# P turned in 32x32 blocks on VectorE and placed by DMAs, in a convolution with 3x3 local attention

## Chip, cores and metric

The kernel runs on one core of a Trainium2 chip. The metric is the device time of one execution in microseconds. A profiled execution gives the span (first to last instruction of the core) and, beside it, its own device time.

## What is computed

The input is a batch of 16 images of 32x32 pixels with 128 channels, float32. Cut to what matters:

```python
perceived = depthwise_conv3x3(x, w_perc) + b_perc        # 3 outputs per channel
hid = gelu(w_up1 @ perceived + b_up1)                    # 256 channels
h = x + w_up2 @ hid + b_up2                              # 128 channels
q, k, v = split(h @ w_qkv.T + b_qkv)
scores[pos] = (q * shifted(k, pos)).sum(-1) * scale      # 9 neighbours, zero padded
w = softmax(scores)
out = h + sum over pos of w[pos] * shifted(v, pos)
```

## The kernel before

**Layout.** An image has 1024 pixels, 8 tiles of 128 pixels (4 rows of 32). The attention of a tile is a dense block: 128 queries on the partitions against a window of 192 keys (the tile's 4 rows and one row above and below), masked. `p_sb` holds exp(scores) for the 8 tiles, [128 queries, 8, 192 keys and a few more], and GpSimd's `normalise` (L918) multiplies half an image (4 tiles, 768 elements a partition) by the reciprocal sums. To multiply by the values, P must have its keys on the partitions: that is `pt`, [128 keys, 8 key tiles, 192 queries that see them].

**P turned.** `transpose_p(n, g)` (L406 to L418) has TensorE transpose the four middle 128x128 blocks of half g into the PSUM bank `work[:, 1 + g]`, and ScalarE's `take_pt` (L579) copies them into `pt`. VectorE's `edges(n, g)` (L781 to L793) turns the 32x32 blocks of the rows above and below, with two STREAM_TRANSPOSE instructions a half. `values(n, g)` (L420) then does 10 matmuls of `v_sb` with `pt` for half an output image, `add_h` (L795) adds h into `o_sb`, and SP stores it.

**Stages.** Each engine runs its own instruction stream, written out by hand, and semaphores order them. `steady` (L224) calls each engine's `body(n, ...)` for n = 0 to 16; five pairs of bodies are a hardware loop. In body n the convolution of image n runs (12 units on TensorE, `unit`, L339, each 9 matmuls of 256 columns), together with the up projection and the attention scores of image n-1, and the values of image n-2. In the code's counting of attention, body n calls `transpose_p(n, 0)` at its end, and body n+1 calls `transpose_p(n, 1)`, `values(n+1, 0)` after unit 0 and `values(n+1, 1)` after unit 1 (L466 to L472). Then come units 2 and 3, the up projection `up` (L365), units 4 and 5, the projections q and v, and units 6 to 11 with the scores between them. Body 16 has no convolution.

**VectorE's order** at the end of a body (L868 to L877): the reciprocal sums of half 1, `edges(n, 0)`, `combine`, `combine_y` and `finish_y` of the second conv half (L718 to L751), `edges(n, 1)`. The gelu on ScalarE waits for `finish_y`. At the start of the next body come `transform_ab`, `add_h` for half 0, `transform`, `add_h` for half 1.

**SP's order** in a body (L301): load the planes of image n+2 when the present ones are used up, load the pixel rows of image n+1 when h of this body is done, and store the two output halves. All its DMAs go through one queue in program order; a wait holds up what stands behind it.

Of the kernel before, what the change touches and what calls it, by code (L numbers as in the profile page):

```python
# [14 lines left out]
P = 128  # L15
# [65 lines left out]

def build(nc, x_planes, x_rows, w_perc, b_perc, w1_c, b_up1, w2_c, b_up2, wqk_c, wv_c, b_qkv, ident_c, ident_bf_c,
          mask_c, zero_c, out):
    with ExitStack() as ctx:
# [13 lines left out]

        ident = sb("ident", [P, P])
        ident_bf = sb("ident_bf", [P, P], BF16)  # L100
# [50 lines left out]


        pt = sb("pt", [P, T, WINDOW])
        o_sb = sb("o_sb", [P, PIX])
# [35 lines left out]
        s_ready = sem("s_ready")  # L190
        pt_ready = sem("pt_ready")
        o_ready = sem("o_ready")
# [5 lines left out]
        p_done = sem("p_done")  # L198
        pt_done = sem("pt_done")

# [10 lines left out]
        rsum_done = sem("rsum_done")  # L211
        edges_done = sem("edges_done")
        pn_last_done = sem("pn_last_done")
# [7 lines left out]
        V_PARTS = (range(0, 2), range(2, 4), range(4, 6), range(6, 8))  # L221
        N_W = 8

        def steady(eng, body, last=None):  # L224
# [42 lines left out]
        @block.sync  # L267
        def _(sp):
            def load(dst, src, **kw):
                sp.dma_start(dst, src, **kw).then_inc(weights_in, 16)  # L270

            def load_planes(n, par):
                sp.dma_start(xp[:, par, :, :, :].rearrange("p k r w -> p (k r w)"), x_planes[n]).then_inc(
                    x_loaded[par], 16)

            def load_rows(n, par):
                sp.dma_start(xr[:, par, :], x_rows[n]).then_inc(xr_loaded[par], 16)

            sp.dma_start(w1T[:, :, :].rearrange("p m d -> p (m d)"), w1_c).then_inc(first_in, 16)
            load_planes(0, 0)  # L280
            sp.dma_start(ident[:, :], ident_c).then_inc(first_in, 16)
            load(w2T[:, :], w2_c)
            load(wqk_in[:, :, :].rearrange("p j c -> p (j c)"), wqk_c)
            load(wv_in[:, :], wv_c)
            load(bqk[:, :], b_qkv[0:2 * C].rearrange("(j p) -> p j", p=P), allow_slow_non_contiguous=True)
            load(bv[:, :], b_qkv[2 * C:3 * C].partition_broadcast(P))
            load(mask_bf[:, :, :], mask_c)
            load(ident_bf[:, :], ident_bf_c)
            load(zeros[:, :, :], zero_c)
            load_planes(1, 1)  # L290
            load_rows(0, 0)
            load_rows(1, 1)

            def store_out(n):
                for g in range(2):

                    sp.wait_ge(o_done, n * 2 - 3 + g)
                    sp.dma_start(out[n - 2][:, g * CH:(g + 1) * CH],
                                 o_sb[:, g * CH:(g + 1) * CH]).then_inc(stored[g], 16)

            def body(n, par, conv, attn, store, more):  # L301
                if conv and (not isinstance(n, int) or n + 2 < B):

                    sp.wait_ge(ab_done, n * 2 + 2)
                    sp.wait_ge(fcge_done, n * 3 + 3)
                    load_planes(n + 2, par)
                if attn and (not isinstance(n, int) or n + 1 < B):

                    sp.wait_ge(h_done, n * 2)
                    load_rows(n + 1, 1 - par)  # L310
                if store:
                    store_out(n)

            steady(sp, body, last=store_out)
            for g in range(2):
                sp.wait_ge(stored[g], 16 * B)

        @block.tensor
        def _(pe):

            def small_weights():
# [9 lines left out]
                pe.wait_ge(biases_in, 48)  # L331
                pe.wait_ge(first_in, 32)
                for g in range(2):
# [71 lines left out]

            def transpose_p(n, g):  # L406
                if is_last(n) and g == 1:
                    pe.wait_ge(pn_last_done, 1)
                else:
                    pe.wait_ge(pn_done, n * 2 + (g - 1))  # L410

                if is_last(n):
                    pe.wait_ge(z_done, n * 4 - 3 if g == 0 else n * 4)
                else:
                    pe.wait_ge(z_done, n * 4 + (0 if g == 0 else -2))
                for u in range(4):
                    last = pe.transpose(work[:, 1 + g, u * P:(u + 1) * P], p_sb[:, 4 * g + u, W:W + P], ident[:, :])
                last.then_inc(pt_ready, 1)  # L418

            def values(n, g):  # L420


                pe.wait_ge(v_done, n * 4 - 4)
                pe.wait_ge(pt_done, n * 2 + (g - 3))
                pe.wait_ge(edges_done, n * 4 + (2 * g - 6))
                half = T // 2 * TR
                blocks = [(i, max(i * TR - 1, g * half), min((i + 1) * TR + 1, (g + 1) * half)) for i in range(T)]
                blocks = [(i, first, end) for i, first, end in blocks if first < end]
                for i, first, end in blocks:
                    above = i * TR - 1  # L430
                    last = pe.matmul(work[:, g, (first - g * half) * W:(end - g * half) * W], v_sb[:, i, :],  # L431
                                     pt[:, i, (first - above) * W:(end - above) * W], start=(i == blocks[0][0]),
                                     stop=(i == blocks[-1][0]), skip_group_check=True)
                last.then_inc(o_ready, 1)

            def last_attention(n):
# [14 lines left out]
                scores(n, 3)  # L451

                transpose_p(n, 0)
                values(n + 1, 0)
                transpose_p(n, 1)
                values(n + 1, 1)

            def body(n, par, conv, attn, store, more):
# [7 lines left out]
                units(0)  # L466
                if store:
                    transpose_p(n - 1, 1)
                    values(n, 0)
                units(1)  # L470
                if store:
                    values(n, 1)  # L472
                units(2)
                units(3)
# [35 lines left out]
                units(9, 10, 11)  # L510
                if attn:
                    transpose_p(n, 0)

# [3 lines left out]
        def _(act):  # L517
# [36 lines left out]
            def prime_gelu():  # L554

                nc.scalar.activation(primer[:, :], ident[:, 0:1], ACT.Gelu).then_inc(primed, 1)

            act.wait_ge(first_in, 32)
            prime_gelu()
# [18 lines left out]

            def take_pt(n, g):  # L579
                act.wait_ge(pt_ready, n * 2 + (g - 1))  # L580
                nc.scalar.copy(pt[:, 4 * g:4 * g + 4, W:W + P],
                               work[:, 1 + g, :].rearrange("p (t q) -> p t q", t=4)).then_inc(pt_done, 1)

            def body(n, par, conv, attn, store, more):
                def exp(i):
                    if i % 2 == 0:
                        act.wait_ge(rmax_done, n * 4 + (i // 2 - 3))
                    u = i % 2 * STEP
                    nc.scalar.activation(p_sb[:, i, 0:KEYS], s_bank(n, i // 2)[:, u:u + KEYS], ACT.Exp,  # L589
                                         bias=negmax[:, i:i + 1], accum_out=p_sum[:, i:i + 1]).then_inc(p_done, 1)  # L590

                if store:
                    take_pt(n - 1, 1)
                if attn:
# [25 lines left out]
                if conv:  # L620
                    prime_gelu()
                if attn:
                    take_pt(n, 0)
                if is_last(n):
                    take_pt(n, 1)

# [3 lines left out]
        def _(dve):  # L630
# [23 lines left out]
            dve.wait_ge(filters_done, 11)  # L654
            dve.wait_ge(first_in, 32)

# [123 lines left out]

            def edges(n, g):  # L781

                if is_last(n) and g == 1:
                    dve.wait_ge(pn_last_done, 1)
                else:
                    dve.wait_ge(pn_done, n * 2 + (g - 1))
                first, end = 4 * g, 4 * g + 4
                a = max(first, 1)
                nc.vector.transpose(pt[P - W:P, a - 1:end - 1, P + W:WINDOW],
                                    p_sb[0:W, a:end, 0:W]).then_inc(edges_done, 1)  # L790
                e = min(end, T - 1)
                nc.vector.transpose(pt[0:W, first + 1:e + 1, 0:W],  # L792
                                    p_sb[P - W:P, first:e, P + W:WINDOW]).then_inc(edges_done, 1)  # L793

# [30 lines left out]
            def body(n, par, conv, attn, store, more):  # L825
# [34 lines left out]
                if is_last(n):  # L860
                    edges(n, 0)
                    sums(n, 1)
                    normalise_last(n)
                    edges(n, 1)
                    add_h(n + 1, 0)
                    add_h(n + 1, 1)
                    return
                if attn:  # L868
                    sums(n, 1)
                    edges(n, 0)  # L870
                if conv:
                    combine(n, 1)
                    combine_y(n, 1)
                if conv:
                    finish_y(n, 1)
                if attn:
                    edges(n, 1)  # L877

# [105 lines left out]
```

## Time and profile before

| what | value |
|---|---|
| median of 3 runs | 500.1 us (498.7 to 500.71) |
| the profiled execution's own time | 498.68 us |
| its span | 496.9 us |
| TensorE matmul busy | 445.7 us, 90% |
| VectorE busy | 356.3 us, 72% |
| ScalarE busy | 230.5 us, 46% |
| GpSimd busy | 194.6 us, 39% |
| DMA queue of SP | 10784 packets, 29.03 MB, 17.4% of 16 engines |

Busy times are sums over the span; matmuls are pipelined, so the rate at which they start says more than how long one lasts. Rows below are read with these names: PE is TensorE's matmul, PEld its weight load, DVE VectorE, ACT ScalarE, POOL GpSimd, SPq the issuing of DMAs by SP. L431 is line 431 of the kernel before.

### The profile page before, as it was taken

The page shows a single profiled execution, that of the slowest core. Times are in us where ns is not written, and L with a number is a line of the kernel's source. Part 1 is how long each engine was busy: PE and PEld are TensorE (multiplying, and loading weights), DVE is VectorE, ACT ScalarE, POOL GpSimd, SP SyncE. Part 2 cuts the span into 40 slices and gives each one's busy share as a digit, 9 for nine tenths or more (in the row PEclk, how much of TensorE's full clock was granted, in tenths as well). Part 3 has the DMA queues.
Part 4 walks back from the last instruction along what each step waited for, and adds up shares of the span by engine and source line. Part 5 has one row for each costly group of instructions (what it writes and reads, how often), then busy time and mean ns, then how long its engine had stood idle before and what let it go on. Part 6 is the DMA issues. An engine that isn't in the chain of part 4 may idle for free.

```text
span 496.9 us, 8443 instructions
## 1 busy us (share of the span) xinstructions
PE 445.7 (90%) x2964; PEld 390.7 (79%) x2964; DVE 356.3 (72%) x728; ACT 230.5 (46%) x491; POOL 194.6 (39%) x154
## 2 busy tenths in 40 slices
PE   1558899999999999999999999999999999999984
PEld 1547588787979788787979788797979888797953
DVE  5997669677685958677685958677685958664644
ACT  2443164453627354453626444453736444461633
POOL 3565435344441525344451526344351526320201
PEclk9999899999999999999999999999999999999999
DMA  8101020303103040402104040402204020201011
GB/s 278 65 0 58 0 100 1 140 2 97 46 13 130 2 142 0 140 0 79 62 3 138 0 140 0 140 0 61 79 0 140 0 84 0 86 2 42 1 44 43
DMA packets 11509, 29.31 MB, mean 59 GB/s; under 512 B 2400, under 2 KB 3168, under 8 KB 11488
## 3 DMA queue, kind: packets, MB, share of 16 engines
q1 hardware_dynamic: 10784, 29.03, 17.4%
q8 instruction: 12, 0.20, 0.2%
q10 hardware_dynamic: 704, 0.02, 0.1%
q14 instruction: 9, 0.07, 0.1%
HBM read 20.65 MB, written 8.39 MB: 58 GB/s over the span
## 4 chain that ended last, share of the span: by engine, by line
PE 61%; DVE 21%; issue 10%; ACT 4%; DMA 1%; DVEq 1%; POOLq 0%; POOL 0%; SPq 0%; ACTq 0%
PE m_ps L359 24%; PE work L372 11%; PE s_ps L401 8%; PE work L431 6%; PE work L378 5%; PE work L383 5%; ACT p_sb L589 3%; DVE y L737 3%; DVE y L740 3%; PE s_ps L397 2%; DVE ps_sb L726 2%; DVE negmax L772 2%; DVE pt L792 2%; DVE o_sb L699 1%; DVE y L736 1%
## 5 line engine op out<-in xcount | busy, mean ns | idle before, releaser
L359 PE MATMUL m_ps<-thi,whi 128*128 128x256 f32 x576 | 187.6, 326 | 14.0 <-POOL wlo L927 6.1
L359 PE MATMUL m_ps<-tlo,whi 128*128 128x256 f32 x576 | 164.2, 285 | 0.0
L359 PE MATMUL m_ps<-thi,wlo 128*128 128x256 f32 x576 | 164.1, 285 | 0.0
L359 PEld LDWEIGHTS m_ps<-thi,whi 128*128 128x128 f32 x576 | 111.3, 193 | 22.5 <-issue 15.1
L918 POOL TENSOR_TENSOR p_sb<-p_sb,rsum 128x768 f32<-128x768 f32 x31 | 45.5, 1468 | 192.7 <-DVE rsum L779 192.7
L359 PEld LDWEIGHTS m_ps<-tlo,whi 128*128 128x128 f32 x576 | 111.6, 194 | 7.2 <-issue 7.2
L359 PEld LDWEIGHTS m_ps<-thi,wlo 128*128 128x128 f32 x576 | 111.4, 193 | 0.0
L911 POOL TENSOR_TENSOR tlo<-t,thi 128x1088 fp32r<-128x1088 f32 (+1 forms) x32 | 61.7, 1948 | 46.1 <-ACT thi L528 46.1
L589 ACT ACTIVATE p_sb<-s_ps,negmax 128x197 f32<-128x197 f32 x124 | 51.4, 423 | 37.6 <-DVE negmax L772 37.6
L606 ACT ACTIVATE q_sb<-work,bq_s 128x512 f32<-128x512 f32 x32 | 22.0, 688 | 100.2 <-PE work L378 100.1
L431 PE MATMUL work<-pt,v_sb 128*128 128x160 f32 (+2 forms) x320 | 50.5, 305 | 17.3 <-DVE pt L792 15.8
L431 PEld LDWEIGHTS work<-pt,v_sb 128*128 128x128 f32 x320 | 47.0, 190 | 20.3 <-issue 20.3
L758 DVE TENSOR_TENSOR v_sb<-work,bv 128x256 f32<-128x256 f32 x62 | 26.1, 421 | 45.2 <-PE work L383 44.9
L372 PE MATMUL work<-hid,w2T 128*128 128x512 f32 x120 | 55.7, 608 | 2.0 <-ACT hid L544 2.0
L544 ACT ACTIVATE hid<-y,b1eff 128x1024 f32<-128x1024 f32 x32 | 36.6, 1144 | 36.9 <-DVE y L750 30.9
L401 PE MATMUL s_ps<-h_around,q_sb 128*128 128x192 f32 x248 | 50.4, 326 | 0.0
L528 ACT CAST thi<-t 128x1088 fp32r<-128x1088 f32 (+1 forms) x32 | 26.3, 870 | 43.6 <-DVE t L677 43.6
L401 PEld LDWEIGHTS s_ps<-h_around,q_sb 128*128 128x128 f32 x248 | 42.2, 191 | 1.4
L372 PEld LDWEIGHTS work<-hid,w2T 128*128 128x128 f32 x120 | 22.2, 194 | 24.7 <-issue 24.7
L821 DVE SCALAR_TENSOR_TENSOR h_around<-work,b,xr 128x512 f32<-128x512 f32 x30 | 22.5, 751 | 20.7 <-PE work L372 20.7
L772 DVE TENSOR_REDUCE negmax<-s_ps 128x2 f32<-128x394 f32 x62 | 35.2, 568 | 2.1
L383 PE MATMUL work<-wvT,h_around 128*128 128x129 f32 x248 | 35.3, 275 | 0.9 <-DVE h_around L821 0.9
(110 smaller groups left out, 665.6 us busy)
## 6 DMA issues: line engine op xcount, KB each, us to landing
xp<-x_planes SPq DMA_DIRECT2D x16, 680.0 KB, 5.6
xr<-x_rows SPq DMA_DIRECT2D x16, 512.0 KB, 4.0
out<-o_sb SPq DMA_DIRECT2D x32, 256.0 KB, 4.1
w1T<-w SPq DMA_DIRECT2D x1, 384.0 KB, 3.2
mask_bf<-masks SPq DMA_DIRECT2D x1, 192.0 KB, 4.0
w2T<-w SPq DMA_DIRECT2D x1, 128.0 KB, 4.9
wqk_in<-w_qk SPq DMA_DIRECT2D x1, 128.0 KB, 4.8
ident<-identity SPq DMA_DIRECT2D x1, 64.0 KB, 4.8
```

Source lines behind the costliest of these rows:

```text
L359: last = pe.matmul(m_ps[:, b, col:col + S], a[:, j, dy, half * P:(half + 1) * P], c[:, par, T_PLACE[j], dy * WIN:dy * WIN + S], start=(s = ...
L372: last = pe.matmul(up_bank(n, c), w2T[:, half * C:(half + 1) * C], hid[:, half, c * CH:(c + 1) * CH], start=(half == 0), stop=(half == 1))
L383: last = pe.matmul(v_bank(n, part)[:, u * VT:(u + 1) * VT], h[:, i * P:(i + 1) * P], wvT[:, :], start=True, stop=True)
L401: last = pe.matmul(s[:, u, 0:WINDOW], q_sb[:, i * P:(i + 1) * P], h_around[:, i * P:i * P + WINDOW], start=False, stop=(u == 1), skip_grou ...
L431: last = pe.matmul(work[:, g, (first - g * half) * W:(end - g * half) * W], v_sb[:, i, :], pt[:, i, (first - above) * W:(end - above) * W] ...
L528: nc.scalar.copy(thi[:, par, part, :], t[:, part, :]).then_inc(thi_done, 1)
L544: nc.scalar.activation(hid[:, half, :].rearrange("p (r k s) -> p k r s", k=K4, s=WIN), y[:, half, :, :].rearrange("p k (r s) -> p k r s", ...
L589: nc.scalar.activation(p_sb[:, i, 0:KEYS], s_bank(n, i // 2)[:, u:u + KEYS], ACT.Exp, bias=negmax[:, i:i + 1], accum_out=p_sum[:, i:i + 1] ...
L758: nc.vector.tensor_tensor(v_sb[:, first:end, :], sums[:, :, 0:C], bv[:, :].unsqueeze(1).to_broadcast([P, len(tiles), C]), ALU.add).then_in ...
L772: nc.vector.tensor_reduce(negmax[:, pair], s[:, :, 0:KEYS], AX.X, ALU.max, negate=True).then_inc(rmax_done, 1)
L911: nc.gpsimd.tensor_tensor(tlo[:, par, part, :], t[:, part, :], thi[:, par, part, :].bitcast(F32), ALU.subtract).then_inc(tlo_done, 1)
L918: nc.gpsimd.tensor_tensor(p_sb[:, tiles, 0:WINDOW], p_sb[:, tiles, 0:WINDOW], rsum[:, tiles].unsqueeze(2).to_broadcast([P, 4, WINDOW]), AL ...
```

## The change

TensorE's transposes, ScalarE's copies and the identity matrix that they needed go. VectorE turns a whole half image (4 tiles, all 192 columns) in one STREAM_TRANSPOSE into a new buffer `turned`. That turns each 32x32 block in place, so the blocks stand on the partitions of their query row and not of their key row. SP then moves them with 12 DMAs a half image, each from 32 partitions of `turned` to 32 partitions of `pt`, in pieces of 32 float32. The turn of half 1 stands between `combine_y` and `finish_y`, and the edges' instructions go. The values stand one conv unit later. In SP's body the moves stand last.

```diff
-        pt_ready = sem("pt_ready")
-        pt_done = sem("pt_done")
-        edges_done = sem("edges_done")
+        turned_done = sem("turned_done")
+        pt_moved = [sem(f"pt_moved{i}") for i in range(2)]
+        MOVED = TR * 3 * 16
...
-            sp.dma_start(ident[:, :], ident_c).then_inc(first_in, 16)
...
+            def move_p(n, g):
+                sp.wait_ge(turned_done, n * 2 + (g - 1))
+                if from_image(n, 2):
+                    sp.wait_ge(o_ready, n * 2 + (g - 3))
+                for row in range(TR):
+                    for dk in range(3):
+                        shift, near = divmod(row + dk - 1, TR)
+                        first, end = max(4 * g, -shift), min(4 * g + 4, T - shift)
+                        col = (near + 2 - dk) * W
+                        sp.dma_start(pt[near * W:(near + 1) * W, first + shift:end + shift, col:col + W],
+                                     turned[row * W:(row + 1) * W, first:end, (row + dk) * W:(row + dk + 1) * W]
+                                     ).then_inc(pt_moved[g], 16)
...
                 if store:
                     store_out(n)
+                if attn:
+                    move_p(n, 0)
+                    move_p(n, 1)
...
             def values(n, g):
                 pe.wait_ge(v_done, n * 4 - 4)
-                pe.wait_ge(pt_done, n * 2 + (g - 3))
-                pe.wait_ge(edges_done, n * 4 + (2 * g - 6))
+                pe.wait_ge(z_done, n * 4 - 4)
+                pe.wait_ge(pt_moved[g], n * MOVED - MOVED)
...
                 units(0)
-                if store:
-                    transpose_p(n - 1, 1)
-                    values(n, 0)
                 units(1)
                 if store:
+                    values(n, 0)
+                units(2)
+                if store:
                     values(n, 1)
-                units(2)
                 units(3)
...
-            def edges(n, g):
+            def turn_p(n, g):
                 (waits for normalise)
+                if from_image(n, 2):
+                    dve.wait_ge(pt_moved[g], n * MOVED - MOVED)
+                tiles = slice(4 * g, 4 * g + 4)
+                nc.vector.transpose(turned[:, tiles, :], p_sb[:, tiles, 0:WINDOW]).then_inc(turned_done, 1)
...
                 if attn:
                     sums(n, 1)
-                    edges(n, 0)
+                    turn_p(n, 0)
                 if conv:
                     combine(n, 1)
                     combine_y(n, 1)
+                if attn:
+                    turn_p(n, 1)
                 if conv:
                     finish_y(n, 1)
-                if attn:
-                    edges(n, 1)
```

ScalarE's exp of the next image waits for `turned_done` where it had TensorE's order before. Three waits for `first_in` go from 32 to 16, because ident isn't loaded.

## Rows read from the trace of the kernel before

**Rows 1.** The page: span, and busy us (share) of each engine.

```profile
span 496.9 us, 8443 instructions
PE 445.7 (90%) x2964; PEld 390.7 (79%) x2964; DVE 356.3 (72%) x728; ACT 230.5 (46%) x491; POOL 194.6 (39%) x154
```

**Rows 2.** Waits: us in total, times, longest us.

```profile
PE work L431 <- DVE pt L792: 15.8, 14, 1.2
```

**Rows 3.** Order of time, TensorE around the values: start, us, what; last row merged.

```profile
302.03 0.60 PE L417 MATMUL work<-ident,p_sb 128*128 128x128 f32 x4
...
303.52 0.60 PE L417 MATMUL work<-ident,p_sb 128*128 128x128 f32 x4
...
303.96 1.50 PE L431 MATMUL work<-pt,v_sb 128*128 128x160 f32 x10
...
305.30 0.36 PE L359 MATMUL m_ps<-thi,whi 128*128 128x256 f32 x1
...
307.74 1.66 PE L431 MATMUL work<-pt,v_sb 128*128 128x32 f32 x10 [1.14 <-DVE pt L792]
...
309.39 2.13 PE m_ps L359 x18
```

**Rows 4.** Order of time, VectorE in the same stretch.

```profile
301.06 0.27 DVE L789 STREAM_TRANSPOSE pt<-p_sb 32x96 f32<-32x96 f32 x1
...
305.94 0.41 DVE L742 SCALAR_TENSOR_TENSOR y<-ru_sb 128x256 f32<-128x256 f32 x1
...
307.32 0.27 DVE L792 STREAM_TRANSPOSE pt<-p_sb 32x96 f32<-32x96 f32 x1
```

**Rows 5.** Groups by line and form: busy us, mean ns, idle before.

```profile
L789 DVE STREAM_TRANSPOSE pt<-p_sb 32x128 f32<-32x128 f32 x16 | 4.9, 304 | 0.5
...
L789 DVE STREAM_TRANSPOSE pt<-p_sb 32x96 f32<-32x96 f32 x16 | 4.3, 272 | 1.4 <-POOL p_sb L918 0.9
```

**Rows 6.** Order of time, SP's issues: start, us in issuing, what.

```profile
5.50 0.43 SPq L270 DMA_DIRECT2D zeros<-zero_keys  x1
5.97 0.43 SPq L273 DMA_DIRECT2D xp<-x_planes  x1
...
315.93 0.35 SPq L277 DMA_DIRECT2D xr<-x_rows  x1
...
344.00 0.35 SPq L277 DMA_DIRECT2D xr<-x_rows  x1
```

**Rows 7.** Issue to landing of the stores (first) and of the row loads.

```profile
DMA to landing us min/median/max: 2.0/4.1/4.7
...
DMA to landing us min/median/max: 3.5/4.0/6.7
```

**Rows 8.** Queues in 0 to 12 us: packets, MB, share of 16 engines.

```profile
q1 hardware_dynamic: 2060, 3.27, 80.8%
q10 hardware_dynamic: 704, 0.02, 3.5%
```

**Rows 9.** Granted clock in 40 slices, then order of time, TensorE in the ramp.

```profile
PEclk9999899999999999999999999999999999999999
...
21.75 0.42 PE L359 MATMUL m_ps<-tlo,whi 128*128 128x256 f32 x1
21.97 0.41 PE L359 MATMUL m_ps<-thi,wlo 128*128 128x256 f32 x1
...
43.65 0.33 PE L359 MATMUL m_ps<-tlo,whi 128*128 128x256 f32 x1
```

**Rows 10.** Order of time, TensorE in the last stages.

```profile
469.11 1.25 PE L417 MATMUL work<-ident,p_sb 128*128 128x128 f32 x8
...
472.78 1.66 PE L431 MATMUL work<-pt,v_sb 128*128 128x32 f32 x10 [0.77 <-DVE pt L792]
...
487.82 0.66 PE L417 MATMUL work<-ident,p_sb 128*128 128x128 f32 x4 [2.03 <-POOL p_sb L918]
...
491.97 1.66 PE L431 MATMUL work<-pt,v_sb 128*128 128x32 f32 x10 [0.72 <-issue]
```

**Rows 11.** Waits in the first 10 us.

```profile
DVE p_sb L690 <- DMA ident<-identity: 1.4, 1, 1.4
```

More of the change, by code:

```diff
@@ L79, in zero_keys, with build @@
     return z
-def build(nc, x_planes, x_rows, w_perc, b_perc, w1_c, b_up1, w2_c, b_up2, wqk_c, wv_c, b_qkv, ident_c, ident_bf_c,
+def build(nc, x_planes, x_rows, w_perc, b_perc, w1_c, b_up1, w2_c, b_up2, wqk_c, wv_c, b_qkv, ident_bf_c,
           mask_c, zero_c, out):
@@ L96, in build @@
         work = psum("work", 3)
-        ident = sb("ident", [P, P])
         ident_bf = sb("ident_bf", [P, P], BF16)
@@ L150, in build @@
         p_sb = sb("p_sb", [P, T, KEYS + 3])
+        turned = sb("turned", [P, T, WINDOW])
         pt = sb("pt", [P, T, WINDOW])
@@ L299, in store_out @@
                                  o_sb[:, g * CH:(g + 1) * CH]).then_inc(stored[g], 16)
+            def move_p(n, g):
[10 more added lines that the diff above has]
+                                     ).then_inc(pt_moved[g], 16)
             def body(n, par, conv, attn, store, more):
+                if isinstance(n, int) and n == 1:
+                    sp.wait_ge(zeroed, 3)
                 if conv and (not isinstance(n, int) or n + 2 < B):
@@ L331, in small_weights @@
                 pe.wait_ge(biases_in, 48)
-                pe.wait_ge(first_in, 32)
+                pe.wait_ge(first_in, 16)
                 for g in range(2):
@@ L404, in scores @@
                 last.then_inc(s_ready, 1)
[L406 to L418, printed above, removed]
             def values(n, g):
                 pe.wait_ge(v_done, n * 4 - 4)
-                pe.wait_ge(pt_done, n * 2 + (g - 3))
-                pe.wait_ge(edges_done, n * 4 + (2 * g - 6))
+                pe.wait_ge(z_done, n * 4 - 4)
+                pe.wait_ge(pt_moved[g], n * MOVED - MOVED)
                 half = T // 2 * TR
@@ L451, in last_attention @@
                 scores(n, 3)
-                transpose_p(n, 0)
                 values(n + 1, 0)
-                transpose_p(n, 1)
                 values(n + 1, 1)
@@ L510, in body @@
                 units(9, 10, 11)
-                if attn:
-                    transpose_p(n, 0)
             steady(pe, body)
@@ L554, in prime_gelu @@
             def prime_gelu():
-                nc.scalar.activation(primer[:, :], ident[:, 0:1], ACT.Gelu).then_inc(primed, 1)
-            act.wait_ge(first_in, 32)
+                nc.scalar.activation(primer[:, :], w1T[:, 0, 0:1], ACT.Gelu).then_inc(primed, 1)
+            act.wait_ge(first_in, 16)
             prime_gelu()
@@ L577, in _ @@
                     nc.scalar.mul(bqk_s[:, :], wa[:, 2 * C + 2:2 * C + 3], -SCALE).then_inc(consts_done, 1)
[L579 to L582, printed above, removed]
             def body(n, par, conv, attn, store, more):
@@ L587, in exp @@
                         act.wait_ge(rmax_done, n * 4 + (i // 2 - 3))
+                        if from_image(n, 2):
+                            act.wait_ge(turned_done, n * 2 + (i // 4 - 3))
                     u = i % 2 * STEP
@@ L590, in exp @@
                                          bias=negmax[:, i:i + 1], accum_out=p_sum[:, i:i + 1]).then_inc(p_done, 1)
-                if store:
-                    take_pt(n - 1, 1)
                 if attn:
@@ L621, in body @@
                     prime_gelu()
[L622 to L625, printed above, removed]
             steady(act, body)
@@ L654, in _ @@
             dve.wait_ge(filters_done, 11)
-            dve.wait_ge(first_in, 32)
+            dve.wait_ge(first_in, 16)
             def rows(a):
@@ L786, in edges @@
                     dve.wait_ge(pn_done, n * 2 + (g - 1))
[L787 to L793, printed above, removed]
+                if from_image(n, 2):
+                    dve.wait_ge(pt_moved[g], n * MOVED - MOVED)
+                tiles = slice(4 * g, 4 * g + 4)
+                nc.vector.transpose(turned[:, tiles, :], p_sb[:, tiles, 0:WINDOW]).then_inc(turned_done, 1)
             def add_h(n, g):
@@ L869, in body @@
                     sums(n, 1)
-                    edges(n, 0)
+                    turn_p(n, 0)
                 if conv:
@@ L873, in body @@
                     combine_y(n, 1)
+                if attn:
+                    turn_p(n, 1)
                 if conv:
                     finish_y(n, 1)
-                if attn:
-                    edges(n, 1)
             steady(dve, body)
@@ L972 @@
     }
-    arrays["identity"] = np.eye(P, dtype=np.float32)
     arrays["identity_bf16"] = np.eye(P, dtype=ml_dtypes.bfloat16)
```

## The prediction

> **What bounds the kernel now.** I read the page's busy shares first: TensorE is busy 90% of a span of 496.9 us, VectorE 72% [rows 1]. Then the waits: in the steady images TensorE idles for one thing only, the values of the second half image (L431), which wait for VectorE's edge transposes (L792) 14 times, 15.8 us in all, 1.13 us a time [rows 2]. The order of time around that wait [rows 3] is the frame for everything below. Call E the end of the last conv unit of an image, 302.03, where the first transpose group starts. From E the old order is: transposes, unit 0, transposes, values 0 (303.96 to 305.30), unit 1, a stall, values 1 at 307.74, which is E+5.71. A unit is half of 2.13 us, 1.065. The period is 344.00 - 315.93 = 28.07 us [rows 6]. So from the start of values 1 to the next E pass 22.36 us.
>
> **TensorE loses work.** Eight transposes an image go, in two groups. From the start of a group to the start of the values behind it are 0.44 us [rows 3], so 0.88 us an image. By the Trainium skill ("VectorE: DVE Perf Modes", The three transpose paths) a 128x128 bf16 transpose takes 390 ns on TensorE, and the page says to use TensorE for a full 128x128 if PSUM will do as its destination. By that figure four would be 1.56 us and an image would save 3.1 us, 2.2 more than by the row, or 36 us less over 16 images. Pipelined behind one another here four take 0.44, so the row decides, and what the change can win on TensorE is small. ScalarE's two copies an image also go; ScalarE is at 46% [rows 1] and I give that nothing.
>
> **What TensorE would want.** Without the groups: units 0 and 1 (2.13), values 0 (1.34), unit 2 (1.065): values 1 could start at E+4.53. After them unit 3 and the rest follow; unit 2 now lies ahead, so 22.36 - 1.065 = 21.30 us remain to the next E. New period = start of values 1 after E, plus 21.30. It stays at 28.07 only if values 1 start by E+6.77.
>
> **VectorE.** Two edge transposes of a half (0.27 + 0.30) become one of 768 elements a partition. By length, 272 ns at 96 elements and 303 at 128 [rows 5] give about 1.03 ns an element, so 768 take 0.96 us; the bounds are 0.30 us (no more than now) and 3.7 us (the four groups of 32 partitions one after the other, where the rows have 32 partitions only). I take 0.96. The first turn starts at 301.06 [rows 4] and ends at E+0.0. Combine and the y parts move 0.35 us later; L742 now ends at 306.35, so the second turn, put ahead of finish_y, runs about 306.7 to 307.6 and ends at E+5.6. That alone is past the E+4.53 that TensorE would want, and no earlier than the edges end now (307.32 + 0.27). Finish_y and the gelu behind it come about 1 us later; TensorE's up wants that gelu only after values 1, so it is covered. VectorE has some 0.8 us more to do in an image, out of the 28% of its time that is idle [rows 1].
>
> **The DMAs.** This is the new path: VectorE, SP's wait, twelve issues, landing, TensorE's wait. All 24 of an image are issued by SP in order. The price of an issue: back to back SP's starts are 0.47 us apart (5.50, 5.97) [rows 6]. Bounds: 0.35, what an issue in the steady images lasts without any gap [rows 6], and 0.60, worked out below. I take 0.47, since the 12 stand back to back as those do. Landing from the issue's start: 2.0 us is the least among the stores, 4.1 their median, 3.5 the least of the row loads [rows 7]. Nothing of SBUF to SBUF is in the trace; a move has 16 KB and the queue holds nothing else then, so I take 2.0, with 1.0 (half the least) and 3.6 as ends. A move is 32 rows by up to 4 tiles in pieces of 128 bytes: 128 pieces, 8 for each of 16 DMA engines. In the first 12 us, 704 small packets took 3.5% of 16 x 12 us, 9.5 ns each, and 2060 mostly larger ones 80.8%, 75 ns each [rows 8]; so the pieces of one move take 0.08 to 0.60 us of each engine, and only at the upper end do they pass the issue.
>
> The sum: SP starts the first half's moves at E+0.2 and issues for 12 x 0.47 = 5.64 us, to E+5.84. The second half, turned at E+5.6, finds SP just done. Its last move is issued at 0.2 + 23 x 0.47 = E+11.0, lands at 13.0, and values 1 start at E+13.1. Period 13.1 + 21.30 = 34.4, **+6.33 us** an image. Values 0 already wait from E+2.13 to about E+7.5, and values 1 again from about E+9.9: two stalls, some 8.6 us together, against 1.13 before. What is queued behind: on TensorE all later units, the up projection and the scores; on SP the next planes' load, issued by E+12 instead of before E, but read by GpSimd only at the next E, over 20 us later, so hidden; rows and stores wait for later events anyway.
>
> Bodies 2 to 15 are 14 such periods: 14 x 6.33 = 88.6. In body 16 (E = 469.11) values 1 start at 472.78 now [rows 10] and at 469.1 + 0.2 + 10.8 + 2.1 = 482.2 then, +9.4, with no unit to hide in. At the very end the first turn starts when the transposes do, 487.82, and ends at 488.8; the moves of both halves follow without a gap, and values 1 start at 488.9 + 10.8 + 2.1 = 501.8 instead of 491.97: +9.8. Together +107.8.
>
> **TensorE's clock.** In the ramp, after a gap of 5.7 us and between short bursts with gaps of 1.6 to 2.7, 256-column matmuls start 0.21 us apart (21.75, 21.97), still so from 40.71 on; at 43.65 the spacing becomes 0.12 [rows 9]. That is 256 columns at 1.2 and at 2.4 GHz, though the page's slices grant it 8 to 9 tenths or more throughout [rows 9]. The late gap of 2.0 us ahead of 487.82 left the pace full [rows 10]. The new stalls are about 5.3 and 3 us with 2.5 us of work between, so I expect the half pace behind them. What lies ahead of the second stall is hidden in it; behind it the row's 2.94 us with 14 matmuls at 0.095 us extra, 1.3 us, for 16 stages: 20.8. Bounds: 0, and 3 us a stage (values, unit 3 and part of up at half pace), 48. The Trainium skill ("TensorE: Matmul & The Clock Gate", HAM oscillation) says that waits on DMA between bursts of matmuls throttle the array again each time; by it the cost is there, without it the sum is 20.8 less.
>
> **Start.** The first weights wait for ident, 1.36 us on VectorE [rows 11]; that load goes. Worth 0 to 1.4, I take 1.0.
>
> Against the profiled execution's 498.7 us (span 496.9; the runs' median is 500.1, 0.3% above, which is not added): 498.7 - 1.0 + 107.8 + 20.8 = **626 us**.
>
> **Rivals.**
> A. The chain through SP as above, but TensorE keeps its full pace: 626 - 21 = 605. For it: the gap of 2.0 us left no trace, and 2.5 us of work lie between the stalls. Against: gaps like 5.7 are followed by half pace.
> B. A move costs 0.60 us, by its pieces or by a dearer issue: values 1 at 0.2 + 23 x 0.60 + 2.1 = E+16.1, +9.33 an image, the two ends +12.4 and +12.8: 498.7 - 1 + 130.6 + 25.2 + 20.8 = 674. A VectorE turn of 3.7 us would put the second turn at about E+11.1 and give a similar time, 5.5 us an image more (some 715).
> C. The other side: the moves are hidden, TensorE gains. It decides at E+6.77: twelve issues and a landing within 1.1 us of the second turn's end at E+5.6. With moves at no cost values 1 start at E+5.7, -1.07 an image, 482; if the turn were early as well, E+4.53, -2.24 an image, 463. For it: TensorE is the bound at 90% and loses work and a stall. Against: one landing is already 2.0 us, and twelve issues 4.2 even at 0.35.
>
> **Numbers.** A change below 0.5% can't be told from none here. Forecast 0.50 (its own range 612 to 645), A 0.22, B and dearer 0.25, C 0.03. The cheap ends of issue and landing together (values 1 at 5.8 + 11 x 0.35 + 1.1 = E+10.8, +4.0 an image, +7 and +4 at the ends), with A, give 565; with one of them cheap it is about 590. The range is 590 to 680, B's 674 within it. Faster 0.02, same 0.01, slower 0.97.
>
> **What would show it.** Right: no L417 and L581; TensorE idle before L431 in two waits an image of about 5.3 and 3 us, released by DMAs into pt; SP issuing 24 moves an image back to back, 0.47 apart; the turns at 0.96; 256-column matmuls at 0.21 spacing after the stalls; a period near 35.7. Wrong: values 1 starting by E+6.8, moves issued much faster than SP's other DMAs, or the time under 590, which would say that issues or landing overlap more than these rows show.

## The result, and the profile after

The changed kernel takes 707.1 us (median of 4 runs, 706.6 to 707.5) against 499.4 us (4 runs) of the kernel before: 1.415 times as long, 95% interval 1.412 to 1.419. Slower was forecast; the size was not: 626 us, range 590 to 680. The profiled execution took 706.75 us. In the experiments below "times before" is the ratio to the kernel before as it ran beside them: 497.1 us beside the fills, the wait for exp and the two kernels with another order, 499.4 us beside the others.

The page of the changed kernel, answering to [rows 1] and to the clock's row of [rows 9] (a line number is from here on that of the kernel whose row it stands in):

```profile
span 704.9 us, 8584 instructions
PE 501.3 (71%) x2836; PEld 440.8 (63%) x2836; DVE 350.5 (50%) x696; ACT 211.7 (30%) x459; POOL 191.5 (27%) x154
PEclk9779888696978979598986979898697968869585
```

No engine is near full any more. TensorE's busy time rose by 56 us although 128 of its matmuls are gone, and its granted clock, full before, dips to 5 to 8 tenths of a slice all through. Its waits (us in total, times, longest), answering to [rows 2], show what it stands for, and one wait that no step of the prediction had:

```profile
PE work L435 <- DMA pt<-turned: 163.1, 32, 12.1
PEld work L435 <- DMA pt<-turned: 68.3, 10, 6.9
...
PEld s_ps L415 <- ACT p_sb L584: 11.9, 11, 1.1
PE s_ps L415 <- ACT p_sb L584: 9.8, 11, 0.9
```

L435 is the values' matmul: 32 waits for the moves, two for each of the 16 images. The second pair of rows says that TensorE waits for exp before the mask matmul of the scores, 11 times; the kernel before did so once.

One image in order of time, TensorE first, answering to [rows 3]; E is 401.94, where unit 0 starts:

```profile
401.94 0.28 PE L377 MATMUL m_ps<-thi,whi 128*128 128x256 f32 x1
...
403.95 0.28 PE L377 MATMUL m_ps<-thi,wlo 128*128 128x256 f32 x1
410.85 2.98 PE L435 MATMUL work<-pt,v_sb 128*128 128x160 f32 x10 [6.61 <-DMA pt<-turned]
...
418.66 2.37 PE L435 MATMUL work<-pt,v_sb 128*128 128x32 f32 x10 [2.76 <-DMA pt<-turned]
...
421.26 0.42 PE L377 MATMUL m_ps<-thi,wlo 128*128 128x256 f32 x1
421.48 0.41 PE L377 MATMUL m_ps<-thi,whi 128*128 128x256 f32 x1
...
422.76 3.65 PE L390 MATMUL work<-hid,w2T 128*128 128x512 f32 x8
...
436.71 0.34 PE L415 MATMUL s_ps<-mask_bf,ident_bf 128*128 128x384 bf16 x1 [0.94 <-ACT p_sb L584]
```

Values 0 wait 6.6 us, values 1 start at E+16.72 (E+13.1 was forecast, E+5.71 before), and the unit behind them has its matmuls 0.21 us apart. VectorE and SP in the same image, answering to [rows 4, 5, 6]:

```profile
400.87 0.98 DVE L779 STREAM_TRANSPOSE turned<-p_sb 128x768 f32<-128x768 f32 x1
...
406.18 0.97 DVE L779 STREAM_TRANSPOSE turned<-p_sb 128x768 f32<-128x768 f32 x1
```

```profile
386.64 0.36 SPq L277 DMA_DIRECT2D xr<-x_rows  x1
...
401.88 15.45 SPq L310 DMA_DIRECT2D pt<-turned  x24
418.00 0.36 SPq L273 DMA_DIRECT2D xp<-x_planes  x1
...
427.38 0.35 SPq L277 DMA_DIRECT2D xr<-x_rows  x1
```

The turns take 0.98 us, as forecast, and end at E-0.1 and E+5.2. SP issues 24 moves without a gap in 15.45 us, 0.644 us each, and the last lands 1.8 us after its issue (all its moves, answering to [rows 7]):

```profile
L310 SPq DMA_DIRECT2D pt<-turned x384: 585/601/742, 74.5 to 696.6; - x192
...
DMA to landing us min/median/max: 1.8/1.8/2.3
```

401.88 + 23 x 0.644 + 1.8 = 418.5, and values 1 start at 418.66. The period is 427.38 - 386.64 = 40.74 us against 28.07 before. Of the 12.7 us, 9.95 are the later values 1 (16.72 + 21.30 - 28.07) and 2.7 come behind them: 1.6 from the slow stretch (418.66 to 422.76 is 4.1 us, the same work took 2.55), 1.1 from the wait before the mask matmul. Other images have a longer slow stretch: from the start of values 1 to the unit behind the up projection the 14 images with a full body take 8.1 us on average, where 6.1 is full pace.

The granted clock of this image shows where the slow stretches stand. It is 1.00 until about 409, some five microseconds into the first wait, and 0.50 from 409.6 to 415.9; that stretch is hidden, because the second half's moves aren't there yet. It is back at 1.00 (0.98) within the second wait, from 416.1 to 419.6, and 0.50 again from 419.8 to 422.8, from about one microsecond after values 1 have started.

### The profile page after: what moved, and what is told of

It is laid out like the page before. It is cut to its first block and busy times, and to the rows that moved or that the text cites. A ratio compares the mean times of both kernels' runs of the same rounds, so it can differ in the third digit from the quotient of the medians.

```text
span 704.9 us, 8584 instructions
## 1 busy us (share of the span) xinstructions
PE 501.3 (71%) x2836; PEld 440.8 (63%) x2836; DVE 350.5 (50%) x696; ACT 211.7 (30%) x459; POOL 191.5 (27%) x154
## 5 line engine op out<-in xcount | busy, mean ns | idle before, releaser
L377 PE MATMUL m_ps<-thi,whi 128*128 128x256 f32 x576 | 199.3, 346 | 15.0 <-POOL wlo L913 7.1
L435 PE MATMUL work<-pt,v_sb 128*128 128x160 f32 (+2 forms) x320 | 92.7, 470 | 163.1 <-DMA pt<-turned 163.1
L435 PEld LDWEIGHTS work<-pt,v_sb 128*128 128x128 f32 x320 | 84.8, 314 | 170.0 <-issue 101.6
L377 PE MATMUL m_ps<-tlo,whi 128*128 128x256 f32 x576 | 174.7, 303 | 0.0
L377 PE MATMUL m_ps<-thi,wlo 128*128 128x256 f32 x576 | 174.0, 302 | 0.0
L377 PEld LDWEIGHTS m_ps<-thi,whi 128*128 128x128 f32 x576 | 122.8, 213 | 23.3 <-issue 14.9
L377 PEld LDWEIGHTS m_ps<-tlo,whi 128*128 128x128 f32 x576 | 123.0, 214 | 7.2 <-issue 7.2
L377 PEld LDWEIGHTS m_ps<-thi,wlo 128*128 128x128 f32 x576 | 122.4, 212 | 0.0
L788 DVE TENSOR_TENSOR o_sb<-work,h_around 128x512 f32<-128x512 f32 x32 | 22.1, 692 | 190.3 <-PE work L435 190.3
```

Of the source, the lines that this page charges most:

```text
L377: last = pe.matmul(m_ps[:, b, col:col + S], a[:, j, dy, half * P:(half + 1) * P], c[:, par, T_PLACE[j], dy * WIN:dy * WIN + S], start=(s = ...
```

## The experiments

**Is it the moves at all?** The values wait for the turn alone, and nothing is moved:

```diff
-                    move_p(n, 0)
-                    move_p(n, 1)
...
-                pe.wait_ge(pt_moved[g], n * MOVED - MOVED)
+                pe.wait_ge(turned_done, n * 2 + (g - 3))
```

> The changed kernel without any move: the values wait for the turn alone and multiply with zeros, all else as in the change. Theory (all that the change costs is the DMAs' chain and the clock behind it): values 1 start just after the second turn's end, E+5.2 to 5.7, the clock stays up, the 1.1 us behind exp stays in ten bodies: 498 - 16 + 11 = 488 to 496 us. Rival (the longer turn on VectorE or the later finish_y cost too): over 500 us.

Measured: 494.0 us, 0.990 times before (0.987 to 0.993). All 213 us between this and the change come with the moves, the clock behind their waits included. The longer turns, the later finish_y and the later gelu cost nothing that shows: the remaining costs are the waits for the second turn, and the same 11 waits for exp as in the change (from its waits; L432 is the values' matmul there).

```profile
PE work L432 <- DVE turned L774: 11.7, 15, 3.1
...
PE s_ps L412 <- ACT p_sb L581: 9.8, 11, 0.9
```

**Count of issues or something else?** Every second move left out:

```diff
+                        if (row + dk) % 2:
+                            continue
                         sp.dma_start(pt[...], turned[...]).then_inc(pt_moved[g], 16)
```

> The changed kernel with every second of the 24 moves an image left out, so half of the blocks never reach the operand of the values. Theory (the chain is the count of issues by SP, 0.644 us each): the first half's six are out before the second turn ends at about E+5.2; values 1 start at E + 5.3 + 5 x 0.644 + 1.8 = 10.3 instead of 16.7, about 6.4 us less an image and 102 over 16: 605 us, and the clock still falls. Rival (the time goes with the landing or with something else than the count): over 670.

Measured: 596.8 us in one run (605 was expected), beside 500.5 of the kernel before. SP's row of one image has twelve issues in 9.09 us, with a pause in them while the second turn ends, and values 1 start at 359.57, 10.5 us after SP's first issue at 349.11:

```profile
349.11 9.09 SPq L312 DMA_DIRECT2D pt<-turned  x12
```

```profile
353.41 0.96 DVE L781 STREAM_TRANSPOSE turned<-p_sb 128x768 f32<-128x768 f32 x1
```

The second turn ends at 354.37, and 354.37 + 5 x 0.64 + 1.8 is 359.4. The chain is the count of issues.

**What makes an issue cost 0.64 us?** Pieces, dimensions and bytes, one at a time, all with 24 moves:

```diff
                         col = (near + 2 - dk) * W
+                        end = first + 1          # one tile; in the second kernel first + 2
```

> All 24 moves, each of one tile in place of up to four: 32 pieces of 128 bytes instead of 128; the other tiles are left out. Theory P (an issue is dearer for its pieces or its third dimension): SP's starts come 0.47 us apart as for its other DMAs, values 1 at E+12.7, 707 - 16 x 4 = 643 us. Theory Q (an issue between SBUF and SBUF costs 0.64 us whatever its shape): spacing 0.64, 705 us.

> All 24 moves, each of two tiles: 64 pieces of 128 bytes, and three dimensions as in the change. If the pieces set the price: spacing between one tile's and four tiles' (0.47 + a third of 0.17, 0.53), 658 us. If the third dimension does: 0.64 as with four tiles, 705 us. If neither: as with one tile.

```diff
-                        sp.dma_start(pt[near * W:..., first + shift:end + shift, col:col + W],
-                                     turned[row * W:..., first:end, (row + dk) * W:(row + dk + 1) * W]
+                        sp.dma_start(<pt rows near, 128 contiguous floats at WINDOW + dk * P>,
+                                     <turned rows row, the first 128 contiguous floats of the half>
```

> All 24 moves with 16 KB each, but as 32 pieces of 512 bytes, contiguous and two-dimensional; they land in parts of pt that are not the right ones. If pieces or dimensions set the price of an issue: spacing as with one tile (0.47), about 643 us. If the bytes do, or it is the price of any such issue: 0.64 and 705 us.

Measured, one run each: 706.6, 707.6 and 707.7 us. SP's row of one image, for one tile, two tiles and long pieces in turn (the second kernel leaves out two of a half's four tiles):

```profile
402.35 15.09 SPq L311 DMA_DIRECT2D pt<-turned  x24
```

```profile
402.56 15.35 SPq L311 DMA_DIRECT2D pt<-turned  x24
```

```profile
403.04 15.09 SPq L310 DMA_DIRECT2D pt<-turned  x24
```

0.63 to 0.64 us whatever the pieces (32 to 128), the dimensions or the bytes (4 to 16 KB). Rival B put such a price down to the pieces or to a dearer issue, without saying what would make one dearer. The pieces fall; the dearer issue stands, and 0.60 us was near. What is left are the two ends of the transfer and the 32 partitions. One kernel takes the source from HBM with all else equal, the other keeps both ends in SBUF and covers 128 partitions:

```diff
-                                     turned[row * W:(row + 1) * W, first:end, ...]
+                                     x_rows[0][row * W:(row + 1) * W, 0:(end - first) * W].rearrange(...)
```

> The changed kernel with the source of each move in HBM (rows of the first image's input) and not in the turned blocks; destinations, shapes and count as in the change; P's blocks are left out. If an issue costs 0.64 us because both sides lie in SBUF: starts 0.47 us apart, values 1 four us earlier, about 645 us. If it costs that because it covers 32 partitions and not 128: 0.64, about 705 us.

```diff
+                        at = row * 3 + dk
+                        sp.dma_start(<pt, all 128 partitions, floats at * W to (at + 1) * W of tiles 4g+1, 4g+2>,
+                                     <turned, all 128 partitions, the same floats of tiles 4g, 4g+1>)
```

> The changed kernel with 24 moves of the same 16 KB from SBUF to SBUF over all 128 partitions, one piece of 128 bytes each, to parts of pt that are not the right ones. If both sides in SBUF set the price of an issue: 0.64, about 705 us. If the 32 partitions do: 0.47, about 645 us. If both kernels, this and the one with the source in HBM, stay at 0.64, then it is neither, and a long row of issues alone has that price.

Measured, one run each: 622.7 us and 709.4 us. SP's rows, source in HBM first:

```profile
358.23 11.26 SPq L310 DMA_DIRECT2D pt<-x_rows  x24
```

```profile
363.12 15.27 SPq L311 DMA_DIRECT2D pt<-turned  x24
```

With the source in HBM an issue costs 0.469 us, which is the 0.47 that the prediction took from loads; from SBUF to SBUF it costs 0.636 over 128 partitions as over 32. The stores settle whether the source alone does it, since they go from SBUF to HBM. In the changed kernel the issues of two stores back to back take 0.91 us together:

```profile
100.39 0.91 SPq L297 DMA_DIRECT2D out<-o_sb  x2
```

So neither end alone makes an issue dear, and the price belongs to having both ends in SBUF. It isn't paid for a queue that has filled up either: the first move behind an idle SP (401.88) already lasts 0.61 us, where the first with its source in HBM (358.23) lasts 0.35. Why two ends in SBUF cost more is not shown. The kernel with cheaper issues is 84 us faster than the change and 22 faster than expected. 23 x 0.175 = 4.0 us for each of 16 images are 64 of the 84; the rest is a shorter stretch at the slow clock (mean granted clock 0.888 against 0.822). From the start of values 1 to the unit behind the up projection its 14 images take 94.2 us against 113.6 in the change. It keeps the 11 waits for exp (9.8 us).

**One engine's sequence, or the transfers?** Every second move goes to ScalarE, behind its exp and its priming of the gelu:

```diff
+                    if (row * 3 + dk) % 2 != share:
+                        continue
...
-                    move_p(n, 0)
-                    move_p(n, 1)
+                    move_p(n, 0, sp, 0)
+                    move_p(n, 1, sp, 0)
...
+                if attn:                        # ScalarE, end of body
+                    move_p(n, 0, act, 1)
+                    move_p(n, 1, act, 1)
```

> The changed kernel with every second move issued by ScalarE, so that SP and ScalarE issue six each for a half. Theory (the chain is the sequence of issues on one engine, not the transfers): the second half's six start at E+5.3 on both and values 1 start at about E+10.5 instead of E+16.7: 600 to 615 us. Rival (both engines' issues share one path behind them, so the pair goes no faster): issues of 1.2 us on each, about 700 us.

Measured: 606.8 us, 1.215 times before (1.208 to 1.223), 100 us faster than the change, with every byte moved. Both engines issue their twelve at the same time, at the price that SP alone had (602 and 622 ns in the median):

```profile
355.91 9.11 SPq L277 DMA_DIRECT2D pt<-turned  x12
```

```profile
356.54 8.80 ACTq L277 DMA_DIRECT2D pt<-turned  x11
```

The transfers had room; the sequence of issues on SP had not. (The second row of ScalarE has 11; its first move is issued at 355.91.) It is still far slower than before: values 1 start at 366.68, 10.8 us after the first issue.

**The clock.** Matmuls in the waits, into banks that the values overwrite:

```diff
+            FILL = (50, 36)
...
+                for _ in range(FILL[g]):
+                    pe.matmul(work[:, g, 0:S], whi[:, 0, 0, 0:P], thi[:, par, 0, 0:S], start=True, stop=True)
                 pe.wait_ge(pt_moved[g], n * MOVED - MOVED)
```

> The changed kernel with 50 matmuls of 256 columns put ahead of the wait of values 0 and 36 ahead of that of values 1, which write the PSUM banks that the values then overwrite; the result is the same. They fill TensorE's two idle stretches. Theory (the stalls let the clock fall, and what comes behind values 1 runs at half pace): the spacing of 0.21 us is gone, values 1 still start at E+16.7, since the DMAs set that, and the stretch behind them is 1.6 us shorter a stage: 707 - 25 = 682 us. Rival (the slower stretch has another cause, such as port contention with the moves): 707 us. If the moves themselves were slowed by the fill, over 707.

Measured: 679.0 us, 1.364 times before (1.360 to 1.368), 28 us less than the change though it computes more. TensorE around the values, with the fills (L432), in one image; SP's first issue is at 387.40:

```profile
389.60 6.10 PE L432 MATMUL work<-thi,whi 128*128 128x256 f32 x50
396.37 1.60 PE L439 MATMUL work<-pt,v_sb 128*128 128x160 f32 x10 [0.68 <-DMA pt<-turned]
...
398.95 4.43 PE L432 MATMUL work<-thi,whi 128*128 128x256 f32 x36
404.09 1.68 PE L439 MATMUL work<-pt,v_sb 128*128 128x32 f32 x10 [0.71 <-DMA pt<-turned]
406.68 3.60 PE L390 MATMUL work<-hid,w2T 128*128 128x512 f32 x8
```

50 matmuls in 6.1 us are at full pace, values 0 take 1.60 us instead of 2.98, and from the start of values 1 to the up projection are 2.59 us instead of 4.10. Values 1 still start 16.7 us after SP's first issue. The mean granted clock is 0.980. By rows: from the start of values 1 to the unit behind the up projection the 14 images take 85.9 us with the fills and 113.6 in the change, 27.7 us, which is the whole gain. The rival, that the moves slow TensorE in another way, is out, since they are all still there.

The Trainium skill ("TensorE: Matmul & The Clock Gate", HAM oscillation) has waits on DMA between bursts of matmuls throttle the array again each time. The change agrees for the first wait, of 6.6 us and more: the values 0 behind it take 2.95 to 2.98 us in all 16 images, against 1.60 here. It isn't each time behind the shorter second wait: with the source in HBM, values 1 run at full pace in 9 of the 14 images, in 1.66 us as at 371.07.

**The wait for exp.** ScalarE's order in the change and before, around the table load of exp:

```profile
434.44 1.28 ACT L584 ACT_TABLE_LOAD   x1 [1.97 <-DVE negmax L761]
435.73 0.43 ACT L584 ACTIVATE p_sb<-s_ps,negmax 128x197 f32<-128x197 f32 x1
```

```profile
321.04 1.28 ACT L589 ACT_TABLE_LOAD   x1
322.95 0.43 ACT L589 ACTIVATE p_sb<-s_ps,negmax 128x197 f32<-128x197 f32 x1 [0.63 <-DVE negmax L772]
```

Before, the 1.28 us table load runs while ScalarE would wait for VectorE's maximum anyway. In the change exp has a second wait (for `turned_done`), and in the ten bodies of the loop the load stands behind the waits (188.31 to 557.20); in the two unrolled bodies ahead of the loop and the three behind it that have both waits it still ran early (as at 105.27 and 637.24). The edit puts that wait ahead of the q projection:

```diff
-                        if from_image(n, 2):
-                            act.wait_ge(turned_done, n * 2 + (i // 4 - 3))
...
+                if attn and from_image(n, 2):
+                    act.wait_ge(turned_done, n * 2 - 2)
                 if attn:
                     for c in range(NCH):
```

> The changed kernel with ScalarE's wait for the turned blocks taken from the exp instructions and put ahead of the q projection, so that exp again has one wait. Theory (the second wait puts the 1.28 us table load for exp behind VectorE's maximum in the ten bodies of the loop, and TensorE's third scores then wait 0.9 us for it): the table load starts before the maximum is there in all bodies, TensorE's wait before the mask matmul of the scores goes in ten bodies, about 1.1 us each, 707 - 11 = 696 us. Rival (that wait is an effect of the half clock pace and of shifted units): the table load moves but TensorE still waits, 705 to 707 us.

Measured: 707.5 us, 1.421 (1.416 to 1.427): no gain. Yet the step itself did what it should:

```profile
433.60 1.28 ACT L582 ACT_TABLE_LOAD   x1
435.51 0.43 ACT L582 ACTIVATE p_sb<-s_ps,negmax 128x197 f32<-128x197 f32 x1 [0.63 <-DVE negmax L761]
```

```profile
PE s_ps L415 <- ACT p_sb L582: 0.5, 1, 0.5
```

Ten of TensorE's eleven waits are gone. The time came back in the slow stretch. The same image shows it at its longest:

```profile
418.44 3.12 PE L435 MATMUL work<-pt,v_sb 128*128 128x32 f32 x10 [3.29 <-DMA pt<-turned]
...
423.27 4.26 PE L390 MATMUL work<-hid,w2T 128*128 128x512 f32 x8
```

Here the granted clock is 0.50 from 418.0 to 424.2, from before values 1 start; in the change it was 0.50 from 419.8 to 422.8. One image could mislead, because in the change values 1 take 2.1 to 2.8 us in some images and 3.1 in others. Over the 14 images, values 1 to the up projection rose from 62.3 to 67.6 us and the up projection from 51.3 to 57.5: 11.5 us in all, as much as the ten waits were worth. With the clock held, both edits in one kernel:

> e1 and e2 together: TensorE's waits filled with matmuls, and exp with one wait. In e1 TensorE's wait for exp went but the half pace lasted longer; with the clock held, theory: the 1.1 us of ten bodies now show, 679 - 11 = 668 us. Rival (moving the wait costs as much elsewhere): 679 us.

Measured: 668.2 us, 1.338 (1.332 to 1.344), 10.8 us less than with the fills alone. The two ran on different chips, and the traces bear it out: between the second halves' values the period is 37.98 us (mean of eight images in the loop) against 39.06, 1.09 us less, and ten bodies make 10.9. The second wait of exp costs 11 us where the clock is steady. In the change alone, taking it away gave nothing, because the slow stretch lengthened by as much; why the clock fell earlier there isn't shown.

**The order alone.** The kernel before with the values one unit later:

```diff
                 if store:
                     transpose_p(n - 1, 1)
-                    values(n, 0)
                 units(1)
                 if store:
-                    values(n, 1)
+                    values(n, 0)
                 units(2)
+                if store:
+                    values(n, 1)
```

> The kernel before with one part of the change alone: the values one conv unit later, transposes and copies as they were. Theory (values 1 wait for VectorE's edges until E+5.71, and a unit ahead of them fills that wait): the 1.13 us stall in 14 bodies goes, the period falls from 28.07 to about 27.0, 499.4 - 15 = 484 us. Rival (what is behind the values, the up projection waiting for o_sb's addition, becomes late instead): 495 to 500 us.

Measured: **485.7 us, 0.975 times before (0.972 to 0.978)**, the fastest here together with the next one. 484 was expected. The wait for the edges, 14 times in [rows 2], is one:

```profile
PE work L431 <- DVE pt L793: 0.8, 1, 0.8
```

The period, from SP's row loads, is 331.68 - 304.67 = 27.01 us; the frame gave 5.71 + 21.30 = 27.01.

```profile
304.67 0.35 SPq L277 DMA_DIRECT2D xr<-x_rows  x1
...
331.68 0.35 SPq L277 DMA_DIRECT2D xr<-x_rows  x1
```

With the second edges ahead of finish_y as well:

```diff
+                if attn:
+                    edges(n, 1)
                 if conv:
                     finish_y(n, 1)
-                if attn:
-                    edges(n, 1)
```

> As b1, and VectorE's second edge transposes put ahead of finish_y, as the change does with its turn. Theory: the edges end 0.65 us earlier, at E+4.9, where TensorE wants them at about E+5.4, so no stall is left: 479 to 482 us. Rival (finish_y and the gelu behind it come 0.6 us later and delay the up projection): equal to b1 or up to 9 us slower.

Measured: 486.3 us, 0.976 (0.971 to 0.981), no different; 479 to 482 was expected. Values 1 start at E+5.47 instead of E+5.70, but TensorE's weight loads now pause 0.84 us within the up projection, at its second half, where they paused 0.57. That half waits for VectorE's addition of values 1 (L803), which ends 9.75 us after E in both kernels. The gain was given back there, by the rows; no run was made to show more.

```profile
302.61 0.30 PEld L372 LDWEIGHTS work<-hid,w2T 128*128 128x128 f32 x2 [0.84 <-issue]
```

## Why the prediction was wrong

- **The frame was right.** The period is the start of values 1 after E plus 21.30 us: with no other cost it gives 27.01 for the order alone, measured 27.01. The rival of hidden moves was priced at 482; without moves the kernel takes 494.0, and the 11 us of the exp wait taken off leave 483. That kernel without the wait was not run.
- **TensorE's and VectorE's terms were right.** Turns of 0.98 us (0.96 forecast), the second ending at E+5.2 (E+5.6), no cost from finish_y that shows.
- **The landing** was 1.8 us (2.0 forecast).
- **The step that failed: "I take 0.47, since the 12 stand back to back as those do."** The rows behind it were loads from HBM. From SBUF to SBUF an issue costs 0.644 us, 4.0 us more over the 23 issues. Values 1 start at E+16.72, 3.6 us later than forecast: 14 x 3.6 and, at the ends, 3.6 and 3.8 more (body 16: +13.0 where +9.4 was taken; the last: +13.6 where 9.8), 58 us. The bound of 0.60 was drawn from the time of pieces on the DMA engines, a mechanism that has no part in it, and held neither the value nor the cause. The sentence "nothing of SBUF to SBUF is in the trace" stood beside the landing; it should have widened the issue's bound too. The range ended at 680, just above B at 0.60, though "B and dearer" had a chance of 0.25 and the prediction's own price of a slow turn was some 715.
- **The clock** was the right mechanism, with a size for another schedule. Forecast were 20.8 us. In the change it costs about 32: 27.7 us in the 14 images, by rows as by the fills, 2.8 us in body 16 (values 1 to the v projection, 663.00 to 671.80, take 8.8 us where 6.0 were needed before) and 1.4 us in the last values (3.11 against 1.66). But at the issue price that was forecast, in the kernel with the source in HBM, the same rows of the 14 images stand only 8.2 us above full pace, where the forecast has 14 x 1.3 = 18.
- **Missed: a wait added to exp**, 11 us. The prediction did not speak of exp's new wait for `turned_done`. The blocks are turned at 407.15 and exp of the next image starts at 435.73, so the wait itself holds nothing up; the cost is in what the second wait displaces, the table load.
- **The start**: the first conv unit begins at 20.36 us instead of 21.40, 1.0 us as forecast; by SP's first row load in the bodies (59.64 instead of 62.36) it is 2.7. Part of that is a difference between executions: the kernel with the order alone starts as the one before does and has that load at 60.80.

In sum 626 + 58 + 11 (clock) + 11 (exp) - 1.7 is 704 us, against 706.75 of the profiled execution; the 2.4 us left aren't explained. That the kernel with the source in HBM took 622.7, near 626, is in part luck: two errors stand against each other in it, the exp wait that was left out and slow stretches shorter than forecast.

## What to carry to other kernels

A chain of DMAs costs its issues one after another on one engine, and a landing once. Count them first: 24 issues of 0.64 us are 15 us, while the eight TensorE transposes that they replace are 0.88. Take a DMA's price only from a row with the same two ends, and where there is none, set its bound wide. When a stall is seen next to a planned change of mechanism, try the reordering by itself: here it alone made the kernel 2.5% faster.

## What the runs showed of the hardware

- A DMA issued by SP in a row with others costs 0.47 us from HBM to SBUF and 0.63 to 0.64 us from SBUF to SBUF, the latter with 32 to 128 pieces, 4 to 16 KB, 32 or 128 partitions alike. Two stores from SBUF to HBM in a row take 0.91 us together. Alone, behind an idle SP, an issue lasts 0.35 us with its source in HBM and 0.61 us from SBUF to SBUF. With half of the moves on ScalarE, SP's issues last 0.60 us (median) and ScalarE's 0.62, against SP's 0.60 alone.
- A move of 4 to 16 KB between SBUF and SBUF lands 1.7 to 1.9 us (medians of the kernels) after the start of its issue.
- A STREAM_TRANSPOSE of 128 x 768 float32 takes 0.98 us; 32 x 128 took 0.30. 272 and 304 ns at 96 and 128 elements on 32 partitions give 0.96 us for 768 elements, so the four groups of 32 partitions are turned side by side.
- With TensorE's waits of 6.6 and 2.8 us in each image, matmuls of 256 columns start 0.21 us apart behind them instead of 0.12 (1.2 GHz instead of 2.4), and the granted clock of the period falls to 0.87. It was back at 1.00 within the second wait and fell once more behind it. Filling the waits with matmuls brings the period to 1.00 and 28 us back.
- A second wait ahead of an activation moves its table load behind both waits in the bodies of the hardware loop; in the unrolled bodies it still ran early.
